# Score layout of the first four heads built on the chip, and GpSimd's opening work reordered, in a one-core attention and expert kernel

## What is computed

```
scale = sqrt(D_K)                                   # 16 heads, D_K 8, D_V 64
q = (ln(x) @ Wq).reshape(B,T,16,8).transpose(0,2,1,3)   # k alike, v with 64
scores = einsum('bhqd,bhkd->bhqk', q, k) / scale    # causal mask: -inf above the diagonal
out = softmax(scores) @ v, heads joined, @ Wo
x = x + out
probs = softmax(ln(x) @ gate_w)                     # 8 experts
top_p, top_idx = top_k(probs over the tokens, 64)   # each expert takes 64 tokens of a batch
x = x + scatter_add(top_idx, top_p * (gelu(xin @ w1) @ w2))
```

## Time and profile before

| | |
|---|---|
| median of 3 runs | 540.45 us (539.96 to 540.6) |
| profiled execution, its own time | 540.85 us |
| its span, first to last instruction | 539.1 us |
| busy: PE / DVE / ACT / GpSimd | 514.4 / 420.4 / 401.1 / 258.4 us |
| first scores of unit 0 start | 20.59 us |
| first scores of unit 1 start | 24.60 us |
| second scores of unit 2 start | 30.64 us |

### The profile page before, as it was taken

The page is one execution under the profiler, slowest core; times in us unless marked ns, Lnnn a source line. Parts: engine busy times, 40 slices in busy tenths (PEclk is TensorE's granted clock), DMA queues, the critical chain, the costliest instruction groups (busy, mean ns, idle before and its releaser), DMA issues.

```text
span 539.1 us, 13960 instructions
## 1 busy us (share of the span) xinstructions
PE 514.4 (95%) x4777; PEld 424.5 (79%) x4777; DVE 420.4 (78%) x1072; ACT 401.1 (74%) x1377; POOL 258.4 (48%) x249
## 2 busy tenths in 40 slices
PE   2599999999999999999999999999999999999996
PEld 1357877878878778788778787777789999999996
DVE  4578888888888888889899999999975587644444
ACT  3589999989999898998989989899743643434330
POOL 5465566565655655565575665557820111011121
PEclk9999999999999999999999999999999999999999
DMA  5484252742644225142350523411300002100002
GB/s 162 140 214 127 73 157 58 236 120 61 166 113 113 80 75 156 29 127 79 80 148 20 149 77 80 134 25 33 107 21 1 2 21 59 36 18 21 11 21 60
DMA packets 49783, 45.97 MB, mean 85 GB/s; under 512 B 4288, under 2 KB 46528, under 8 KB 49728
## 3 DMA queue, kind: packets, MB, share of 16 engines
q1 hardware_dynamic: 48768, 44.54, 30.3%
q10 hardware_dynamic: 960, 0.72, 0.5%
HBM read 26.35 MB, written 18.89 MB: 84 GB/s over the span
## 4 chain that ended last, share of the span: by engine, by line
PE 87%; DVE 5%; ACT 3%; issue 2%; DMA 1%; ACTq 1%; POOLq 0%; POOL 0%; DVEq 0%
PE ctx_ps L1198 16%; PE t_ps L1285 10%; PE misc_ps L1207 10%; PE t_ps L1171 5%; PE t_ps L1181 5%; PE t_ps L1172 5%; PE misc_ps L1117 4%; PE s_ps L1269 4%; PE misc_ps L1119 3%; PE misc_ps L1118 3%; PE s_ps L1157 3%; PE s_ps L1270 3%; PE s_ps L1271 3%; PE s_ps L1144 3%; PE s_ps L1153 2%
## 5 line engine op out<-in xcount | busy, mean ns | idle before, releaser
L558 ACT ACTIVATE prob<-s_ps,neg_max 128x128 f32<-128x128 f32 (+1 forms) x512 | 208.7, 426 | 5.5 <-DVE neg_max L1033 1.6
L493 POOL TENSOR_TENSOR probn<-prob,inv 128x1024 f32<-128x1024 f32 x64 | 121.3, 1895 | 54.8 <-DVE inv L1013 53.2
L558 ACT ACTIVATION_READ_ACCUMULATOR prob<-s_ps,neg_max 128x1 f32 x512 | 108.3, 212 | 0.0
L486 POOL TENSOR_TENSOR probn<-prob,inv 128x512 f32<-128x512 f32 x64 | 66.7, 1042 | 63.6 <-PE t_ps L1181 57.4
L606 ACT ACTIVATE hT<-s_ps 128x512 f32<-128x512 f32 x64 | 38.0, 598 | 64.3 <-PE s_ps L1271 61.8
L949 DVE TENSOR_REDUCE neg_max<-s_ps 128x4 f32<-128x1024 f32 x63 | 75.2, 1194 | 1.7 <-PE s_ps L1157 1.6
L517 POOL TENSOR_TENSOR y_parts<-y_sb,y_parts 128x512 fp32r<-128x512 f32 x16 | 21.2, 1328 | 106.9 <-ACT y_parts L616 106.9
L1207 PE MATMUL misc_ps<-wo_sb,ctxT 128*128 128x128 f32 x512 | 67.8, 275 | 0.9 <-DVE x_all L768 0.9
L1207 PEld LDWEIGHTS misc_ps<-wo_sb,ctxT 128*128 128x128 f32 x512 | 62.2, 192 | 1.3 <-issue 1.3
L1171 PE MATMUL t_ps<-ident,probn 128*128 128x128 f32 x256 | 61.9, 282 | 0.0
L1172 PE MATMUL t_ps<-ident,probn 128*128 128x128 f32 x256 | 60.1, 275 | 0.0
(11 more groups left out here) (184 smaller groups left out, 1168.2 us busy)
## 6 DMA issues: line engine op xcount, KB each, us to landing
qT<-q_rows SPq DMA_DIRECT2D x15, 512.0 KB, 4.0
q_rows<-qk_hi SPq DMA_DIRECT2D x32, 128.0 KB, 2.4
q_rows<-qk_lo SPq DMA_DIRECT2D x32, 128.0 KB, 2.4
k_diag_odd<-k_rows SPq DMA_DIRECT2D x32, 128.0 KB, 4.3
k_rows<-qk_hi SPq DMA_DIRECT2D x30, 128.0 KB, 2.4
k_rows<-qk_lo SPq DMA_DIRECT2D x30, 128.0 KB, 2.4
k_diag_even<-k_rows SPq DMA_DIRECT2D x28, 128.0 KB, 4.3
w_raw<-in_L_ffn_w SPq DMA_DIRECT2D x1, 2048.0 KB, 9.8
```

The lines of the kernel that those rows point to most:

```text
L486: nc.gpsimd.tensor_tensor(probn[r][:, 0:HG * P].rearrange("p (i k) -> p i k", i=HG), prob[r][:, 0:HG * P].rearrange("p (i k) -> p i k", i=HG),
L493: nc.gpsimd.tensor_tensor(probn[r][:, HG * P:].rearrange("p (i k) -> p i k", i=HG), prob[r][:, HG * P:].rearrange("p (i k) -> p i k", i=HG ...
L558: last = nc.scalar.activation(prob[r][:, first + i * keys:first + (i + 1) * keys], scores[:, i, :], ACT.Exp, bias=neg_max[:, r, block_, i: ...
```

## The change

Group 0 of batch 0 no longer goes through HBM. ACT and DVE copy the weights of the first four heads four times side by side (`own_w_hi`, `own_w_lo`, kept in `k_diag[1]`'s group 0 until it is zeroed), and `own_queries_keys` makes the queries and keys of these heads with the repeated weights, so they come out in the score layout, in `misc_ps[1]`. `split_own` on DVE turns them into hi and lo rows: with `is_low` 0 or 1 and `hi_sign` 1 or -1 by partition (`sign_copies`), the row is `own * is_low + hi * hi_sign`. The loads of group 0 (one of 128 KB, four of 32 KB) go away, and ACT's two loads are now of groups 1 to 3. The scores of unit 0 come ahead of the values and of batch 1's transposes, and `misc_ps[1]` is used beside `misc_ps[0]`. GpSimd makes the mask tables before batch 1's `norm1_scale` and zeroes groups 1 to 3 of `k_diag[1]`, which DVE did. ACT zeroes groups 0 and 3 of `k_diag[0]`, DVE 1 and 2; `wv_hi` moves ahead of `qk_hi`.

```diff
                 if b < RING:
-                    sp.wait_ge(zeroed, 3 + 4 * b)
+                    sp.wait_ge(zeroed[b], 3 + b)
                 await_count(sp, s1_done, G * (b - 1))
                 if b == 0:
-                    load_rows(b, slice(0, 1), first_loaded, range(2))
-                    load_rows(b, slice(1, G), qk_loaded)
+                    load_rows(b, slice(1, G), qk_loaded, range(2))
...
+            mask_shapes()
             norm1_scale(0)
+            pool.wait_ge(rstd1_done, 1)
+            half_products()
             norm1_scale(1)
-            masks()
+            for j in range(1, G):
+                nc.gpsimd.tensor_scalar(k_diag[1][:, j, :, :].rearrange("p i t -> p (i t)"),
+                                        eps_sb[:, 0:1].broadcast_to([P, HG * T]), 0.0, None, ALU.mult).then_inc(zeroed[1], 1)
...
+            def repeat_weights():
+
+                act.wait_ge(w_hi, 2)
+                for w in range(2):
+                    nc.scalar.activation(own_w_hi[:, w, :].rearrange("p (i r d) -> p i r d", i=HG, r=4),
+                                         bcast(f32(wqk_hi[:, w, 0:HG * DK]).rearrange("p (i d) -> p i d", i=HG), 2, 4),
+                                         ACT.Copy).then_inc(own_w, 1)
...
+            repeat_weights()
             split_norms(0, 0)
-            zero_keys(0, range(2))
+            zero_keys(0, 0, zeroed_own)
+            act.wait_ge(wv_loaded, 16)
+            nc.scalar.activation(wv_hi[:, :], wv_raw[:, :], ACT.Copy).then_inc(w_hi, 1)
             split_qk(0)
             act.wait_ge(qk_hi_done, 1)
             store_rows(act, qk_hi, K_HI)
             act.wait_ge(qk_lo_done, 1)
             store_rows(act, qk_lo, K_LO)
-            act.wait_ge(wv_loaded, 16)
-            nc.scalar.activation(wv_hi[:, :], wv_raw[:, :], ACT.Copy).then_inc(w_hi, 1)
-            split_norms(1, 1)
-            act.wait_ge(qk_stored, QK_STORES)
-            act.wait_ge(zeroed, 3)
-            for i in range(2, HG):
-                act.dma_start(f32(k_diag[0][i * ROWS:(i + 1) * ROWS, 0:1, i, :]),
-                              k_rows.rearrange("(j i) r d t -> i (r d) j t", j=G)[i][:, 0:1, :]).then_inc(first_loaded, 16)
-            copy_values(0, 0, 0)
-            copy_values(1, 1, 0)
+            zero_keys(0, 3, zeroed[0])
+            split_norms(1, 1, misc_ps[1])
             act.wait_ge(max0, 1)
             exps(0, 0, s0_ps, P, 0, exp0)
-            split_qk(1)
+            act.wait_ge(qk_stored, QK_STORES)
+            act.wait_ge(zeroed[0], 3)
+            for i in range(2, HG):
+                act.dma_start(f32(k_diag[0][i * ROWS:(i + 1) * ROWS, 1:G, i, :]),
+                              k_rows.rearrange("(j i) r d t -> i (r d) j t", j=G)[i][:, 1:G, :]).then_inc(qk_loaded, 16)
+            copy_values(0, 0, 0)
             act.wait_ge(max1, 1)
             exps(0, 1, s1_ps, T, HG * P, exp1)
+            split_qk(1)
+            copy_values(1, 1, 0, misc_ps[1])
...
+            def split_own():
+
+                dve.wait_ge(own_done, 1)
+                dve.wait_ge(signs, 3)
+                for w in range(2):
+                    nc.vector.tensor_scalar(own_hi[:, w, :], own_ps[:, w, :], hi_sign[:, w:w + 1], None,
+                                            ALU.mult).then_inc(own_hi_done, 1)
+                dve.wait_ge(own_hi_done, 2)
+                dve.wait_ge(zeroed_own, 1)
+                nc.vector.scalar_tensor_tensor(out=qT[0][:, 0, :], in0=own_ps[:, 0, :], scalar=is_low[:, 0:1],
+                                               in1=f32(own_hi[:, 0, :]), op0=ALU.mult, op1=ALU.add)
+                for i in range(HG):
+                    rows = slice(i * ROWS, (i + 1) * ROWS)
+                    last = nc.vector.scalar_tensor_tensor(out=k_diag[0][rows, 0, i, :], in0=own_ps[rows, 1, :],
+                                                          scalar=is_low[rows, 1:2], in1=f32(own_hi[rows, 1, :]),
+                                                          op0=ALU.mult, op1=ALU.add)
+                last.then_inc(own_ready, 1)
...
             split_qk_weights()
+            repeat_weights()
+            split_norms(0, 0)
             dve.wait_ge(x_loaded[1], 16)
             norm_stats(lambda tb: x_all[:, TB + tb, :], bn6, mv1, bn1_done, 2, stats1)
-            split_norms(0, 0)
+            zero_keys(0, 1)
             zero_keys(0, 2)
             split_qk(0)
-            zero_keys(0, 3)
+            split_own()
             norm1(1)
-            zero_keys(1, 0)
+            dve.wait_ge(s0_done, 1)
+            nc.vector.tensor_reduce(out=neg_max[:, 0, 0, :], in_=s0_ps[:, :, :], axis=AX.X, op=ALU.max, negate=True).then_inc(max0, 1)
             dve.wait_ge(w_hi, 3)
             nc.vector.tensor_tensor(wv_lo[:, :], wv_raw[:, :], f32(wv_hi[:, :]), ALU.subtract).then_inc(w_lo, 1)
-            split_norms(1, 1)
-            for j in range(1, G):
-                zero_keys(1, j)
-            dve.wait_ge(s0_done, 1)
-            nc.vector.tensor_reduce(out=neg_max[:, 0, 0, :], in_=s0_ps[:, :, :], axis=AX.X, op=ALU.max, negate=True).then_inc(max0, 1)
+            split_norms(1, 1, misc_ps[1])
             dve.wait_ge(s1_done, 1)
             nc.vector.tensor_reduce(out=neg_max[:, 0, 1, :], in_=s1_ps[:, :, :], axis=AX.X, op=ALU.max, negate=True).then_inc(max1, 1)
             dve.wait_ge(exp0, 1)
             nc.vector.reciprocal(inv[:, 0, 0, :], sums[:, 0, 0, :]).then_inc(inv0, 1)
             nc.vector.tensor_copy(s0_ps[:, :, :], bcast(causal[:, :], 1, HG)).then_inc(filled0, 1)
-            split_qk(1)
+            zero_keys(1, 0)
+            dve.wait_ge(exp1, 1)
+            nc.vector.reciprocal(inv[:, 0, 1, :], sums[:, 0, 1, :]).then_inc(inv1, 1)
             dve.wait_ge(s0_done, 2)
             nc.vector.tensor_reduce(out=neg_max[:, 1, 0, :], in_=s0_ps[:, :, :], axis=AX.X, op=ALU.max, negate=True).then_inc(max0, 1)
-            dve.wait_ge(exp1, 1)
-            nc.vector.reciprocal(inv[:, 0, 1, :], sums[:, 0, 1, :]).then_inc(inv1, 1)
+            split_qk(1)
...
+            def own_queries_keys():
+
+                pe.wait_ge(own_w, 4)
+                for w in range(2):
+                    last = split_product(own_ps[:, w, :], own_w_hi[:, w, :], own_w_lo[:, w, :],
+                                         xT_hi[0][:, :], xT_lo[0][:, :])
+                last.then_inc(own_done, 1)
...
+                        if at(u, (0,)):
+                            pe.wait_ge(qk_lo_done, 2)
...
             queries_keys(0)
+            own_queries_keys()
             nc.tensor.matmul(s0_ps[:, :, :], ident_bf[:, :], bcast(causal[:, :], 1, HG), start=True, stop=True)
-            pe.wait_ge(qk_lo_done, 1)
-            turn_first_norms(1)
-            pe.wait_ge(w_hi, 3)
-            pe.wait_ge(w_lo, 3)
-            pe.wait_ge(xT_ready, 2)
-            values(0, 0)
-            pe.wait_ge(v_ready, 1)
-            values(1, 0)
-            pe.wait_ge(v_ready, 2)
-            pe.wait_ge(first_loaded, QK_LOADS)
+            pe.wait_ge(own_ready, 1)
             first_scores(0, 0)
             pe.wait_ge(halves, 10)
             second_scores(0, 0)
+            turn_first_norms(1, misc_ps[1])
+            pe.wait_ge(w_hi, 3)
+            pe.wait_ge(w_lo, 3)
+            pe.wait_ge(qk_lo_done, 1)
+            values(0, 0)
+            pe.wait_ge(xT_ready, 2)
+            values(1, 0, misc_ps[1])
+            pe.wait_ge(v_ready, 1)
             queries_keys(1)
             pe.wait_ge(qk_loaded, QK_LOADS)
             pe.wait_ge(filled0, 1)
             first_scores(1, 0)
-            pe.wait_ge(qk_lo_done, 2)
```

63 lines of the change are left out of this document (42 added, 21 removed).

## The result

The changed kernel takes 535.96 us (median of 4 runs, 535.00 to 536.63) against 540.53 for the kernel before on the same chip: ratio 0.9915, 95% interval 0.9903 to 0.9927, or 4.6 us less. A second set on another chip gave 536.08 (6 runs, 534.96 to 536.51) against 540.57, ratio 0.9915 [0.9900, 0.9929]. The profiled execution took 535.0, its span is 533.3. The forecast of 536.1, and its range, hold. Not every step behind them does, and two of its errors cancel.

The account below looks back on a forecast made before the run. TensorE bounds the steady part, a chain jumping between engines the opening. 7.0 sooner at unit 0's first scores, minus 3.6 (loads), plus 0.8 (stages no longer waiting in turn) gives 4.2: 536.25, leaning 0.1 for the clock to 536.1; range 534.7 to 538.0.

Parts of the forecast that it names:

- The yardstick: Unit 2's second scores, after which TensorE has hardly a gap: at 26.4 instead of 30.64, 4.2 us sooner.
- signs of being wrong: Split past 14.2, load landing after 4, batch 1's rstd1 past 15, DVE longer beside zeroing, clock step over 2 from 33.
- TensorE near 7.95: Start of the first products of queries and keys: near 7.95 us, not 8.24, as xT_lo begins 0.2 to 0.3 sooner.
- 7 x 0.39: DVE's split_own: seven instructions of 0.39, 2.7 us, ready at 13.45 after overlap and wait; unit 0's first scores 7.0 sooner.
- Only then ACT issues its two loads: ACT's loads go out behind unit 0's four exponentials, at 17.7 and 18.1, landing at 21.3 or 21.1.
- At most 1.90: Each of GpSimd's three zeroings: at most 5.7 us plus stalls together, ending about 20, costing nothing unless over 4 each.
- GpSimd pays, DVE doesn't: When both engines work at once, only GpSimd's instructions lengthen; DVE's zeroing keeps 0.74 and wv_lo 1.23.
- The rival's price of 2.2: GpSimd holds up DVE's split_own, xn and wv_lo by 2.2 us: gain 2.0, time 538.4; chance 0.06.
- Masks by 12.6, expected 11 to 12: GpSimd's mask tables, begun at 5.4: end at 12.6 at the old price of 7.1 us, expected 11 to 12.
- clock near 33: TensorE's rise from 1.2 to 2.4 GHz comes 4.2 us earlier, to about 33, with the steady work.
- the rival of an early rise: TensorE's clock rises already in the denser opening: gain 4.2 + 1.3 = 5.5, time 535.0; chance 0.18.
- They had 3 us of slack: Batch 1's loads come 3.4 us sooner, their use 4.2 sooner; with 3 us of slack they stay hidden.

Follow-up runs that it names:

- run 9: The changed kernel, unchanged, measured again on another chip: 536.08 us, ratio 0.9915.
- run 5: The changed kernel with the six own products of the first half of the heads done twice: 537.50 us, ratio 0.9945.
- run 10: The changed kernel with GpSimd's three zeroings back on DVE and unit 0's four keys' blocks made by copies: 536.14 us, ratio 0.9917.
- run 3: The changed kernel with GpSimd's three zeroings back on DVE: 535.69 us, ratio 0.9913.
- run 4: The changed kernel with GpSimd beginning its three zeroings only when split_own is done: 536.32 us, ratio 0.9926.
- run 11: The changed kernel with zeroings on DVE and constant products in TensorE's gaps, 13 before the split's wait, 3 more behind batch 1's transposes: 534.79 us, ratio 0.9894.
- run 12: The changed kernel with zeroings on DVE, keys' blocks by copies and TensorE's gaps filled, 11 products before the split's wait: 535.58 us, ratio 0.9907.
- run 7: The changed kernel with products of two constants put into TensorE's gaps in the opening: 535.82 us, ratio 0.9915.
- run 1: The kernel before with only GpSimd's new order (masks first, three zeroings), none of the layout: 540.51 us against 540.31, ratio 1.0004.
- run 2: The changed kernel with the mask tables behind both norm1_scale, as before the change: 536.62 us, ratio 0.9935.

## Why the forecast was right, point by point

- *Place and size.* The yardstick came at 26.43 (forecast 26.4), the second maxima at 23.2 (23.3), unit 1's first scores at 21.32 (21.2). The time followed, since TensorE has hardly a gap behind it, with the exception of unit 4 in the kernels with a larger lead. Part of the hit is luck: three of the forecast's own signs of being wrong came (a split that ends behind 14.2, `xn` longer beside GpSimd in one execution, and a step of the clock more than 2 us from 33 in the other), and the sign of being right that was to tell the mechanism, a wait for ACT's last load ahead of unit 1's first scores, did not.
- *"TensorE near 7.95":* 8.32 here, behind the weights' load, which landed 0.4 later than before; 8.06, 7.92 and 8.02 in runs 9, 5 and 10. Right but for the landing.
- *"7 x 0.39":* the failed term of the split. 3.3 instead of 2.55, beyond even its upper bound. Each of the seven takes 0.46 to 0.50, and the four that write 32 partitions start 0.48 to 0.50 apart, that is, without the overlap that had been taken off. Runs 3 and 4 show that this is their own price. Unit 0's scores came 6.0 sooner, not 7.0.
- *"Only then ACT issues its two loads":* wrong. They went out 0.7 sooner than forecast, beside the exponentials, landed some 3.5 later (the median of the two), and TensorE did not wait for them: it was busy itself until 21.3. What made it so late is the split: unit 0's scores 1.04 later than forecast, `wv_lo` done at 17.25 and not 16.3, the values from 17.35 and not 16.4. The late split and this error cancelled: a split of 2.55 with loads at 21.2 gives the same 21.2. Runs 10 to 12 show the other side: with TensorE sooner, the loads are the wait, as the forecast had drawn it, but the last is SP's, bound by the stores' end and not by ACT's exponentials.
- *"At most 1.90" for a zeroing on GpSimd:* 2.97. The cover held: they end at 19.9, the first `probn` begins at 20.65 and nothing waits for it.
- *"GpSimd pays, DVE doesn't":* wrong in the second half. `xn` 1.43, a zeroing 1.51, `wv_lo` 1.93 beside GpSimd's long instructions, against 0.60, 0.68 and 1.22. The rival's price of 2.2 was not paid, since one instruction of the chain at a time was caught: in the changed kernel `xn` kept its 0.60 in one execution and took 0.97 in the other, and from unit 0's scores to the values it was 2.76 and 2.90; in runs 4, 5 and 7 it was 3.3 to 3.4.
- *Masks by 12.6, expected 11 to 12:* 9.6, 4.2 us in place of 7.1; little fell beside DVE's zeroing.
- *"From the products to the yardstick", clock near 33:* the level rose between 22.0 and 23.4 in both executions, fell at 26, and rose again at 29.6 in the one and 32.7 in the other. So the condition of the rival of an early rise came in both, and it gave nothing by itself, because DVE and ACT set the distance from unit 1 to unit 2; what gave 1.2 is that the second rise came 3 us sooner, close to the forecast's price of 1.0 to 1.4 for 4 us. The forecast had no fall and second rise in it. Two profiles don't tell how much of the runs' spread of 1.6 us this is; the kernel before, which shows no early rise in its trace, spreads by 2.5 in the 17 runs beside which runs 1 to 4 were measured.
- *"They had 3 us of slack", of batch 1's loads:* true at 4.2 of lead; at 5.7 in run 7 it is spent, and in run 5, whose stores are later too, already at 3.9. So the forecast's "no wait later in the kernel is tied to an absolute time" holds for the changed kernel, not for all of these.

## What to carry to other kernels

Taking a wait out of a chain of engines gives only what the next resource allows: here 7.0 forecast at the first scores, 6.0 had, 4.2 kept, because TensorE's own order (the values now stand between unit 0's scores and unit 1's, and wait for `wv_lo`) and a load were ready to be the next wait within half a microsecond of each other. Before speeding up one link further, find that second wait: run 10 saved 0.4 us in the split and kept none, and the load that stopped it was not the one that had been suspected, so look up which of several issues landed last. Not tried was `wv_lo` ahead of the first maxima, which by the rows is the wait of the values. Where a saved microsecond also shifts the clock, compare several executions and read the lead unit by unit, since one execution can show 1.2 us that is no part of the order.
